# Waiting for landed gathers twice a round, in a two-layer graph kernel on one core

## What is computed

```python
# layer 0
xs_e, xv_e = xs[src], xv[src]
out_s = f(xs_e * es, xv_e . ev)          # with W_ss, W_vv
out_v = g(xs_e * ev, xv_e * es)          # with W_sv, W_vs
messages = concat(out_s, out_v) * sigmoid(edge_scalars @ W_rad.T + b_rad)
agg = segment_sum(messages, dst)
x = layernorm(x + linear(x + agg))
# layer 1
w = silu(edge_scalars @ Wfc1) @ Wfc2
mid = w * products(f0[src], f1[src], edge_attr_sh)
n = segment_sum(mid, dst) / count
x = layernorm(x + sc(x) + alpha(n) * conv(n))
```

## Time and profile before

| | us |
|---|---|
| median of 3 runs | 5404.95 (5401.82 to 5424.09) |
| the profiled execution | 5458.66 |
| its span, first to last instruction | 5456.8 |

### The profile page before, as it was taken

How to read it: one execution, slowest core, us unless ns; L and a number is a source line. 1 busy time by engine, 2 the same in 40 slices (tenths; PEclk the granted TensorE clock), 3 DMA queues, 4 the chain that set the end, 5 groups by cost and what they waited for, 6 DMA issues and landing times.

```text
span 5456.8 us, 61361 instructions
## 1 busy us (share of the span) xinstructions
PE 4384.4 (80%) x12412; PEld 2659.6 (49%) x12413; DVE 3868.2 (71%) x8785; ACT 2607.9 (48%) x8195; POOL 3314.4 (61%) x3267
## 2 busy tenths in 40 slices
PE   6778677777777777777878988888888888888887
PEld 4555455555555455555644444444444444444445
DVE  4777777777777777776757666767666667667677
ACT  3444444444544545444544444444444444444444
POOL 4666666666666666666356666666666656666661
PEclk7555555555555555555788988999999989999898
DMA  7555555555555555555323223323322323223231
GB/s 241 154 155 158 148 155 153 149 154 155 155 153 155 147 154 158 152 156 151 102 80 83 81 77 83 82 80 82 81 81 80 82 76 83 81 80 81 79 83 52
DMA packets 245760, 640.14 MB, mean 117 GB/s; under 512 B 57085, under 2 KB 95407, under 8 KB 245627
## 3 DMA queue, kind: packets, MB, share of 16 engines
q0 software_dynamic: 181152, 556.66, 37.5%
q1 hardware_dynamic: 64576, 83.11, 5.1%
HBM read 618.66 MB, written 20.88 MB: 117 GB/s over the span
## 4 chain that ended last, share of the span: by engine, by line
DVE 33%; PE 29%; another core or an unknown queue 18%; issue 11%; ACT 5%; DVEq 3%; DMA 1%; ACTq 0%; POOL 0%; SPq 0%; POOLq 0%
PE ps L963 17%; DVE work L675 9%; DVE work L658 6%; DVE onehot L708 5%; PE ps L956 5%; ACT work L470 4%; PE ps L950 3%; PE ps L943 2%; DVE acc L715 2%; DVEq L772 1%; DVE work L653 1%; DVE work L663 1%; DVE work L664 1%; DVE work L695 1%
## 5 line engine op out<-in xcount | busy, mean ns | idle before, releaser
L373 POOL DMA_INDIRECT work<-table,srcs x1596 | 1633.9, 1024 | 936.5 <-issue 790.7
L373 POOL DMA_INDIRECT arena<-table,srcs x1596 | 1603.4, 1005 | 940.9 <-issue 893.2
L963 PE MATMUL ps<-arena,onehot 128*128 128x161 f32 x3608 | 1065.6, 475 | 643.3 <-DVE arena L681 532.7
L963 PE MATMUL ps<-work,onehot 128*128 128x384 f32 x3608 | 1381.2, 532 | 82.7 <-DVE work L702 64.9
L963 PEld LDWEIGHTS ps<-arena,onehot 128*128 128x128 f32 x3608 | 912.0, 317 | 970.3 <-issue 958.3
L470 ACT ACTIVATE work<-work,harm 128x96 f32<-128x96 f32 (+1 forms) x3224 | 1070.4, 416 | 24.9 <-DVE work L702 14.1
L470 ACT ACTIVATE work<-arena,harm 128x160 f32<-128x160 f32 (+1 forms) x3224 | 984.8, 389 | 96.5 <-DVE arena L681 77.9
L963 PEld LDWEIGHTS ps<-work,onehot 128*128 128x128 f32 x3608 | 702.3, 204 | 657.6 <-issue 305.9
L943 PE MATMUL ps<-wrad,escal 49*128 49x320 f32 x1612 | 918.7, 716 | 0.0
L956 PE MATMUL ps<-fc,hid 128*128 128x384 f32 x1612 | 656.3, 533 | 285.7 <-ACT hid L560 208.9
L498 ACT ACTIVATE ps<-ps 128x640 f32<-128x640 f32 x403 | 276.9, 687 | 1194.2 <-PE ps L943 534.7
(11 more groups left out here) (127 smaller groups left out, 2488.6 us busy)
## 6 DMA issues: line engine op xcount, KB each, us to landing
escal<-in_escal SPq DMA_DIRECT2D x404, 98.0 KB
arena<-table,srcs POOLq DMA_INDIRECT x1596
work<-table,srcs POOLq DMA_INDIRECT x1596
table<-work SPq DMA_DIRECT2D x49, 224.0 KB, 4.8
dst_sh<-in_dst_sh SPq DMA_DIRECT2D x52, 160.0 KB
table<-work SPq DMA_DIRECT2D x7, 784.0 KB, 4.0
acc<-in_xd SPq DMA_DIRECT2D x1, 3920.0 KB
arena<-in_xd SPq DMA_DIRECT2D x7, 560.0 KB, 4.2
```

What stands on the lines that cost most here:

```text
L373: pool.indirect_dma_start(out=rows[:, j, t, :], out_offset=None, in_=table, in_offset=bass.IndirectOffsetOnAxis(ap=of[:, j, t:t + 1], axis ...
L963: last = mm(bank(to)[:, 0:(MSG0, MSG1)[l]], onehot[:, b, t, :], m[:, j % 2, t, :], start=t == 0, stop=t == TPS - 1)
```

## The change

`gathers_of_round` gets one more wait. For j = 0 and j = 2 (PAIR is 2) GpSimd waits, after the waits that were there, for the landing of the slot that it filled just before: for j = 0 that is slot 3 as filled in the round before (a count of 64 r), for j = 2 slot 1 as filled in this round (64 (r + 1)). Nothing else changes. The gathers of the first round, which come from `lists`, don't wait.

```diff
                         pool.wait_ge(s_wtd[l], s + 1)
                         pool.wait_ge(s_wone[l], s + 1)
+                        if j % PAIR == 0:
+                            pool.wait_ge(s_rows[l][(j - 1) % SLOTS], (r + (1 if j else 0)) * 16 * TPS)
                         pool.sem_inc(s_pool, 1)
                         gather(l, j, srcs[:, b, :, :])
```

## The result

The changed kernel takes **5548.64 us** (median of 4 runs, 5543.55 to 5555.52), the kernel before in the same comparison 5410.53 us (5401.82 to 5424.09): a ratio of 1.0254, 95% interval 1.0227 to 1.028, or +138 us. A second comparison gave 5542.26 us and 1.0243 [1.0226, 1.026]. The forecast was 5525 us, slower, in a range from 5300 to 5600.

The account below looks back on a forecast made before the run. It took GpSimd's issuing plus one pause a round as the bound. Layer 0's +134 us and layer 1's -12 us gave +122 us on 5458.66 us, scaled by 1.0% to +121 us, or 5525 us; range 5300 to 5600 us.

Parts of the forecast that it names:

- The old pauses: GpSimd's stops before gathers, about 4.6 us a round, 462 us in layer 0 and 458 in layer 1, expected to go.
- The sigmoid's prompt start: Expected in the changed profile: ScalarE's sigmoid starts within 0.1 us of its radial product's end whenever ScalarE waits.
- The turn of the loop: One round before: 16 gathers (20.6 us), 2.4 us to VectorE's add, 1.7 us of VectorE, 0.78 us until GpSimd starts.
- The price of a wait: Per new GpSimd wait: landing (2.5 us layer 0, 1.75 layer 1) plus restart 0.78 us, less the 0.30 us gap.
- the regular gap of 0.30 us: GpSimd's idle time between two gathers inside a run, 479 us for 1596 gathers.
- The issue time of a gather: GpSimd's time per gather, means 1.005 us in layer 0 and 1.024 us in layer 1, assumed unchanged.
- the first rival: Waits end sooner and GpSimd's gathers issue faster, so faster than before: -136 us, about 5270 us; chance 0.18.
- the sum on the profile: Both layers' new pauses less old ones, +122 us, added to the profiled execution of 5458.66 us, before scaling.
- Late signals beside the new waits: Rival: TensorE's signals late in runs of eight too, a quarter of old pauses (230 us) remaining: about 5750 us; chance 0.07.
- a clock that falls in layer 1: Rival: TensorE's clock drops to half in a quarter of layer 1's rounds, costing 235 us: about 5760 us; chance 0.05.
- No change: Rival: new pauses only replace old ones, +54 us in layer 0 and -52 in layer 1: 5405 us; chance 0.15.
- to wait late: Skill rule: issue a DMA early and wait late to overlap its fixed cost; the change does the opposite 400 times.

Follow-up runs that it names:

- run 4: Kernel before the change, no new wait, with the third and fourth gather of each supertile left out after the first round: 4364.05 us, ratio 0.8084.
- run 2: Changed kernel with one wait a round instead of two, before the first supertile only: 5340.52 us, 0.9897 of the kernel before.

## Why the prediction was right

**The mechanism.** The old pauses were said to come from signals of TensorE that are held while a long run of gathers lasts. Half the gathers took the late signals away (run 4), runs of 16 brought them back at the forecast place, prompt at 12.2 us and late at 17.0 us (run 2), and runs of eight with a stop of 1.9 us or more have hardly any. The sigmoid's prompt start could not be read in the changed kernel as the prediction wanted: ScalarE comes to its sigmoid from a wait for rows, and by then TensorE is long done. What shows it is that 403 sigmoids waited 7.9 us in all, and that the largest row of "remote" is 5.1 us.

One reading was too strong, that signals late in a run come only when the gathers have landed. In the very run that the prediction reads, a third product lies between its two:

```profile
1206.37 2.50 PE L943 MATMUL ps<-wrad,escal 49*128 49x320 f32 x4
...
1210.91 0.69 ACT L498 ACTIVATE ps<-ps 128x640 f32<-128x640 f32 x1 [3.74 <-remote]
```

It ends at 1208.87, 12.3 us into the run, and its sigmoid starts 2.0 us late, while GpSimd issues on until 1217.12. So between prompt and held lies a stretch with some signals late by less. The turn of the loop has a slip too: VectorE's add came 1219.61 - 1217.12 = 2.5 us after the run, not 2.4.

**The price of a wait.** 3.28 us (2.5 + 0.78) and 2.53 us (1.75 + 0.78) were forecast, 655.2 / 198 = 3.31 and 512.1 / 197 = 2.60 us measured. In the rows shown a landing is 2.26 to 2.48 us in layer 0 and 1.76 in layer 1, the restart 0.75 us. The Trainium skill, "DMA: Bandwidth & Descriptors", section "Anatomy of one DMA — SWDGE (gpsimd) path", by which these landings were estimated at 1.6 and 1.3 us after the issue, is too low here by 0.5 to 0.9 us.

**Two terms were mis-sized, in opposite directions.** Beside the waits, the idle time before a gather was taken at the regular gap of 0.30 us. In the changed kernel layer 0's idle time less its 198 waits is (1116.3 - 655.2) / 1398 = 0.33 us for each other gather, and layer 1's (970.9 - 512.1) / 1399 = 0.33 us. The usual gap is still 0.30 us, as the timeline above shows; the rest is longer pauses that the forecast had put at nothing. With layer 1's somewhat dearer waits this makes idle times of 1116 and 971 us where 1075 and 925 were forecast, 41 and 46 us too few. The issue time of a gather, which was left as it is, fell from 1.005 to 0.992 us and from 1.024 to 0.972 us, 102 us in all: this is the part of the first rival that came true, at half of what it had at most (203 us). The median stayed, and in layer 1 the longest got shorter (1808 to 1433 ns), as line 373 alone shows beside the earlier trace rows (min/median/max in ns):

```profile
L373 POOL DMA_INDIRECT arena<-table,srcs x1596: 941/949/1686, 95.5 to 2788.6; - x200
L373 POOL DMA_INDIRECT work<-table,srcs x1596: 948/957/1433, 2937.4 to 5456.3; - x200
```

Counted over the two traces, gathers longer than 1.1 us fell from 308 to 197 in layer 0 and from 220 to 38 in layer 1: fewer are held up. Which work held them up no run shows; the shortening comes with the stops (layer 1's gathers take 0.972 us with layer 1's waits alone, 1.027 us with layer 0's alone), and the prediction, which saw no reason that pauses at new places change how many are held up, was wrong in that.

**The sum.** Between the two profiled executions +122 us was forecast and +97 measured (5555.52 - 5458.66), so the sum on the profile, 5581 us, was 25 us too high. Then the prediction scaled everything down by 1%, 56 us, because the profiled execution of before lay 1% above its median; the changed kernel's lay only 0.1%, 7 us, above. The two errors work against each other, and that the forecast of 5525 us came out only 24 us low is in part luck. New pauses should not have been scaled with the old ones: layer 1 with two full drains has a round of 25.2 us in four profiles, without a stop one of 25.2 to 26.3 us. The two comparisons of the changed kernel (5549 and 5542 us) don't show this, since the kernel before took 5410 us in both.

**The rivals.** Late signals beside the new waits, and a clock that falls in layer 1, did not come: "remote" and the clock's row show it. "No change" was nearly true of layer 1 by the difference of +138 and +140 us, and not on the chip where its waits alone won 1.3%. The rule of the Trainium skill that was weighed, "DMA: Bandwidth & Descriptors", section "Rules for kernel authors", to wait late, agrees with the four waits (+22%) and with the change; it doesn't with the kernels whose layer 0 waits for three gathers of four, just as early, and which are 2.3 to 4.9% faster than the one that never waits.

**What stays open.** Which path of the chip TensorE's signals share with the gathers, if they share one; whether the length of the stop counts or how long the DMA engines rest in it (with three of four, layer 0's stop of 1.9 us with a rest of 1.3 to 1.4 us is enough and layer 1's of 1.3 us with a rest of 1.4 to 1.5 us is not, which speaks for the length, but the layers differ in row size too); and why one long and one short stop in turn nearly suffice in layer 1 (2.6 and 1.3 us) but not in layer 0 (1.9 and 0.7).

## What to carry to other kernels

Before a wait is added, price it from two rows, the landing of what it waits for and the restart of the engine that waits, and multiply; the price of a wait so read was within 3% here, and it showed which layer would lose. It does not scale with the old pauses. When a signal's consumer starts microseconds after the producer's end, look at what else is in flight: short stops in a long series of transfers can cost less than the late signals that they prevent, and the length of the stop has to be measured for each transfer size. The kernel bound by late signals differed by 2% between chips here, so compare within one chip.

## What the runs showed of the hardware

TensorE's signals reached ScalarE promptly early in a run of gathers (gathers less than 0.6 us apart) and late in a long one. Counted over layer 0 of the kernel before, for the sigmoids before which ScalarE stood idle: 111 of 119 started within 0.15 us when their product ended in the first 8 us of a run, 58 of 87 when it ended between 8 and 14 us, and none of 65 between 16 and 18 us. With one wait a round it was 83 of 89, 82 of 110, and none of 47. In the run shown of that kernel the late signal came 5.7 us after its product, 2.15 us after the run's last issue.

In layer 0 a stop of 1.9 us every eight gathers is enough (24.2 us for a round) and one of 0.7 us is not (25.2 us); GpSimd need not wait for the last landing, but at the stops that are enough the gathers' DMA queue does run dry, for a median of 1.3 to 1.4 us. The kernel without stops has medians 2% apart on different chips (5397 to 5508 us). The one with two full drains took 5542 and 5549 us where that kernel took 5410 both times, so whether it varies less from chip to chip is not shown by its time.
